# Splitting the attention output on ScalarE and VectorE instead of GpSimd

## The reference, cut to what matters

```python
x = x + cross_attention(layernorm(x), ctx)       # 16 heads, 8192 keys
x = x + self_attention(layernorm(x))             # 16 heads, causal, rotary
x = x + experts(layernorm(x))                    # top 4 of 32, and a shared one

def self_attention(x):                           # x: (512, 512)
    q, k, v = split(x @ w_qkv)                   # 16 heads of 32
    q, k = rotate(q), rotate(k)
    attn = softmax(where(causal, q @ k.T / sqrt(32), -inf))
    out = attn @ v
    return out @ w_o
```

## Time and profile before

| | |
|---|---|
| median of 3 executions | 1501.06 us (1498.43 to 1502.47) |
| the profiled execution, its own time | 1501.06 us |
| its span, first to last instruction | 1499.7 us |
| busy: PE / DVE / ACT / POOL | 95% / 77% / 68% / 42% of the span |
| the chain that ended last, by engine | PE 75%, POOL 10%, DVE 6%, issue 4%, ACT 3%, DMA 2% |
| the units of stage three in the trace | 1208.6 to 1286.2 us |
| product with w_o | from 1288.9 us |

### The profile page before, as it was taken

How to read it: one execution, slowest core, us unless ns; L and a number is a source line. 1 busy time by engine, 2 the same in 40 slices (tenths; PEclk the granted TensorE clock), 3 DMA queues, 4 the chain that set the end, 5 groups by cost and what they waited for, 6 DMA issues and landing times.

```text
span 1499.7 us, 24614 instructions
## 1 busy us (share of the span) xinstructions
PE 1419.0 (95%) x8812; PEld 778.5 (52%) x8812; DVE 1150.2 (77%) x2814; ACT 1017.3 (68%) x1318; POOL 632.5 (42%) x426
## 2 busy tenths in 40 slices
PE   7999999999999976999999999999999899999993
PEld 5866666666666643444444443444443765744441
DVE  6878787887778775899999989998988767533334
ACT  5577777777777775988888888888898446211221
POOL 0199787777787981131152323110000211154551
PEclk9999999999999998999999999999999999999997
DMA  5464344433343235854455444456451340257994
GB/s 197 133 235 155 127 157 165 152 133 128 127 144 138 100 117 162 214 131 116 113 122 129 116 120 112 124 123 169 119 130 40 108 169 1 116 216 271 410 406 175
DMA packets 94574, 229.45 MB, mean 153 GB/s; under 512 B 12737, under 2 KB 13130, under 8 KB 91638
## 3 DMA queue, kind: packets, MB, share of 16 engines
q1 hardware_dynamic: 88288, 218.37, 46.1%
q0 software_dynamic: 5600, 8.42, 1.6%
q10 hardware_dynamic: 566, 1.09, 0.2%
HBM read 171.15 MB, written 64.91 MB: 157 GB/s over the span
## 4 chain that ended last, share of the span: by engine, by line
PE 75%; POOL 10%; DVE 6%; issue 4%; ACT 3%; DMA 2%; SPq 0%; POOLq 0%; ACTq 0%; DVEq 0%
PE PS L796 18%; PE PS L817 15%; PE PS L319 9%; PE PS L323 8%; PE PS L278 5%; PE PS L1623 4%; PE PS L1640 2%; POOL W_ L610 2%; POOL kr L609 2%; POOL kr L612 2%; POOL R L601 2%; PE PS L1582 2%; DVE rel L586 2%; PE PS L825 2%; PE PS L1199 2%
## 5 line engine op out<-in xcount | busy, mean ns | idle before, releaser
L850 ACT ACTIVATE P<-PS 128x1024 f32<-128x1024 f32 x512 | 480.5, 1040 | 81.7 <-PE PS L796 77.9
L586 DVE CUSTOM_DVE_ANT_0 rel<-PS,rel 128x256 f32<-128x256 f32 x1024 | 363.2, 420 | 109.0 <-PE PS L278 105.9
L910 DVE TENSOR_TENSOR W_<-W_,P 128x2048 f32<-128x2048 f32 x108 | 255.2, 2423 | 12.9 <-ACT P L850 12.9
L910 DVE TENSOR_TENSOR acc<-acc,P 128x2048 f32<-128x2048 f32 x108 | 245.4, 2330 | 18.9 <-ACT P L850 18.7
L817 PE MATMUL PS<-P,qe 128*32 128x512 f32 x2048 | 257.0, 600 | 0.7 <-ACT on L873 0.7
L323 PE MATMUL PS<-Wh,R 128*128 128x512 f32 x512 | 180.3, 415 | 0.0
L438 ACT ACTIVATE rel<-PS 128x1024 f32<-128x1024 f32 x128 | 131.5, 1028 | 71.7 <-PE PS L278 71.5
L319 PE MATMUL PS<-R,Wh 128*128 128x512 f32 x512 | 175.6, 414 | 4.1 <-ACT kr L405 4.1
L444 ACT ACTIVATE rel<-PS 128x1024 f32<-128x1024 f32 x128 | 131.5, 1028 | 45.8 <-PE PS L278 45.2
L278 PE MATMUL PS<-khd,qh 32*128 32x256 f32 x2048 | 130.4, 327 | 24.3 <-DVE mpart L586 9.4
L278 PEld LDWEIGHTS PS<-khd,qh 32*128 32x128 f32 x2048 | 79.6, 183 | 123.1 <-issue 81.5
(11 more groups left out here) (304 smaller groups left out, 2078.3 us busy)
## 6 DMA issues: line engine op xcount, KB each, us to landing
khd<-kscr SPq DMA_DIRECT2D x129, 256.0 KB, 4.1
y<-in_y SPq DMA_DIRECT2D x16, 1024.0 KB, 5.4
vscr<-W_ SPq DMA_DIRECT2D x16, 1024.0 KB, 5.0
kscr<-khd SPq DMA_DIRECT2D x16, 1024.0 KB, 7.0
kscr<-kl SPq DMA_DIRECT2D x16, 1024.0 KB, 5.1
qe<-vscr SPq DMA_DIRECT2D x64, 256.0 KB, 2.7
kl<-kscr SPq DMA_DIRECT2D x63, 256.0 KB, 4.2
Wp<-in_w_e SPq DMA_DIRECT2D x6, 1536.0 KB
```

The source lines that it names most:

```text
L586: last = dve.tensor_tensor_reduce(out=rel[i][:, j, t, :], in0=PS[:, 2 * b + j, t * 256:(t + 1) * 256], in1=rel[i][:, j, t, :], scale=1.0, ...
L850: act.activation(P[s % 4][:, 2 * pr:2 * pr + 2, :], PS[:, 2 * b:2 * b + 2, :], ACT.Exp, scale=SCALE).then_inc(exp_done, 1)
L910: dve.tensor_tensor(a[:, :, :], a[:, :, :], P[s % 4][:, :, :], ALU.add).then_inc(summed, 1)
```

## The change

ACT and DVE take over what POOL did for `at_`, and ACT the copies of `w_o`. POOL keeps the four subtractions for `w_o`. ACT now makes the copy for group g at the end of unit 3g + 5 (u = 5, 8, 11), after `take_turned(u - 1)`, and one copy of `w_o` at the end of each of the units 3 to 6, behind the former. DVE makes the subtraction for group g at the end of the same unit, after `empty_turned(u - 1, 0)`, and waits there for ACT's copy. The semaphore `split3` goes; PE waits for `at_low` at 3 and at 4 instead.

```diff
 # third_pe
-        pe.wait_ge(split3, 6)
+        pe.wait_ge(at_low, 3)
         pe.wait_ge(w_lows, 12)
...
-        pe.wait_ge(at_low, 1)
+        pe.wait_ge(at_low, 4)
 # third_act
             if u:
                 take_turned(u - 1)
+            if u > 2 and u % 3 == 2:
+                high_attention(u // 3 - 1)
+            if 2 < u < 7:
+                if u == 3:
+                    act.wait_ge(qw_in, 48)
+                    act.wait_ge(side_made, SIDE["project", 2, 3] + 1)
+                act.copy(R[2][:, u - 3, :], W0[0][:, u - 3, :]).then_inc(wo2_high, 1)
         act.activation(dmy[:, 1:2], epst[:, 0:1], ACT.Sqrt)
         take_turned(11)
         take_shares(3)
-        act.wait_ge(at_done, 4)
-        act.copy(R[0][:, 3, :], at_[:, 3, :]).then_inc(at_high, 1)
+        high_attention(3)
...
+    def high_attention(g):
+        act.wait_ge(at_done, g + 1)
+        act.copy(R[0][:, g, :], at_[:, g, :]).then_inc(at_high, 1)
 # third_dve
             if u:
                 empty_turned(u - 1, 0)
+            if u > 2 and u % 3 == 2:
+                low_attention(u // 3 - 1)
         empty_turned(10, 1)
         empty_turned(11, 0)
         empty_turned(11, 1)
         weighted(3)
-        dve.wait_ge(at_high, 1)
-        dve.tensor_tensor(R[1][:, 3, :], at_[:, 3, :], R[0][:, 3, :].bitcast(F32), ALU.subtract).then_inc(at_low, 1)
+        low_attention(3)
...
+    def low_attention(g):
+        dve.wait_ge(at_high, g + 1)
+        dve.tensor_tensor(R[1][:, g, :], at_[:, g, :], R[0][:, g, :].bitcast(F32), ALU.subtract).then_inc(at_low, 1)
 # third_pool
-        pool.wait_ge(qw_in, 48)
         for k in range(4):
-            pool.tensor_copy(R[2][:, k, :], W0[0][:, k, :]).then_inc(wo2_high, 1)
             pool.wait_ge(wo2_high, k + 1)
             pool.tensor_tensor(R[3][:, k, :], W0[0][:, k, :], R[2][:, k, :].bitcast(F32), ALU.subtract).then_inc(w_lows, 1)
-        for g in range(3):
-            pool.wait_ge(at_done, g + 1)
-            pool.tensor_copy(R[0][:, g, :], at_[:, g, :]).then_inc(split3, 1)
-            pool.wait_ge(split3, 2 * g + 1)
-            pool.tensor_tensor(R[1][:, g, :], at_[:, g, :], R[0][:, g, :].bitcast(F32), ALU.subtract).then_inc(split3, 1)
 # fourth_sp
-        sp.wait_ge(at_low, 1)
+        sp.wait_ge(at_low, 4)
```

More of the change, by code:

```diff
@@ L1058, in program @@
     xT2_dve = sem("xT2_dve")
-    w_lows, split3 = sem("w_lows"), sem("split3")
+    w_lows = sem("w_lows")
     pair_in = [sem(f"pair_in{i}") for i in range(11)]
```

## The result

| | before | after |
|---|---|---|
| median | 1500.37 us (6 runs) | 1515.22 us (6 runs, 1513.55 to 1516.36) |
| ratio, 95% interval | | 1.0099 (1.0087 to 1.0112) |
| profiled execution, its own time | 1501.06 us | 1515.08 us |
| span | 1499.7 us | 1513.7 us |
| mean granted clock of TensorE | 0.983 | 0.976 |

The change makes the kernel about 1% slower, 14.85 us by the medians. The forecast was slower, but by 5.05 us.

A forecast was written before the change was run, and what follows sets the result against it. PE was taken as the bound, busy 16.36 of 16.70 us. Two turns at 1.84 plus 1.37 at the end gave 5.05 us on 1501.06, so 1506.1 us; 8-in-10 range 1502.0 to 1508.8.

The forecast's parts named there:

- Value: The worth set on each part in stage three: POOL's relief 0, ACT's added copies 0.
- Sum: The total over two turns and the end of unit 11: 2 x 1.84 + 1.37 = 5.05 us slower.
- Nothing gained from GpSimd's relief: POOL loses 8.1 us of copies and subtractions before unit 11 ends; nobody waited for them, so 0.
- POOL's work was slowing DVE: Rival: if all 8.1 us of POOL came off DVE's path, 3.1 us net gain, 1498.0 us; chance 4%.
- ScalarE's copies at units 3, 4 and 6: 0: At these unit ends copies push exponentials by up to 0.62 us, which ACT's idle time takes up: 0.
- VectorE's wait and the steps behind it: DVE waits for ACT's late copy ahead of the maxima: 1.84 us at turns 5-6 and 8-9, 1.37 after unit 11.
- The lock with GpSimd: At unit 5 a POOL subtraction could hold up DVE's new one by at most 1.3 us once; taken as 0.
- The delays are not taken up: Against the rival that DVE's waits fall into idle time at the turns: 1501.7, up to 1503.5 us; chance 17%.
- The clock: Rival: PE's gaps bring one clock fall before the product with w_o, 2.5 us more, 1508.6 us; chance 13%.
- The range: The forecast's own range for the whole kernel, 1505 to 1507.8 us, given 60%.

The follow-up runs named there:

- fill_exact: Changed kernel with short fp32r filler products on TensorE that end within its three new gaps; 1504.77 us, ratio 1.0034.
- copy_early: Changed kernel with ScalarE's copy of at_ in units 5, 8 and 11 moved ahead of raise_scores(u, 0); 1500.07 us, ratio 0.9997.
- weight_only: Kernel before with only the four copies of w_o moved to ScalarE, everything for at_ as before; 1499.52 us, ratio 1.0000.
- pool_late: Kernel before with GpSimd's key-weight subtractions held until VectorE's last step of the first normalisation is done; 1501.87 us, ratio 1.0010.
- low_later: Changed kernel with VectorE's subtractions moved behind shift(6, 1), shift(9, 1) and the last copies of turned blocks; 1502.00 us, ratio 1.0008.
- attention_only: Changed kernel with GpSimd keeping its four copies of w_o, so only the at_ work moves; 1512.00 us, ratio 1.0088.
- fill_end: Changed kernel with float32 filler products on TensorE only in the gaps behind unit 11; 1513.03 us, ratio 1.0073.
- wait_only: Kernel before with only a VectorE wait for ScalarE's take_turned(u - 1) at the ends of units 5 and 8; 1502.33 us, ratio 1.0015.
- both: Kernel before with the edits of norm_fill and pool_late together; 1502.83 us, ratio 1.0021.
- norm_fill: Kernel before with fp32r filler products on TensorE in the gaps of the first normalisation; 1500.40 us, ratio 1.0003.

## Why the prediction was wrong

The direction was right, and so was the mechanism of the 5 us that it forecast. Two thirds of the slowdown came by another way, and there one step failed: "Value" and "Sum" took a gap on PE to cost its own length, and left the clock to a rival with 13% and one fall of 2.5 us, "in front of the product". The runs showed three falls, worth 10.2 us beside 4.97 us of lateness (fill_exact).

- **Nothing gained from GpSimd's relief.** Right: copy_early leaves it the whole relief of 8.1 us and stands at 0.9997, weight_only the relief of four copies and stands at 1.0000. The rival "POOL's work was slowing DVE" is refuted.
- **ScalarE's copies at units 3, 4 and 6: 0.** Right within what can be measured (weight_only).
- **VectorE's wait and the steps behind it: 1.84 a turn, 1.37 at the end.** Right. The wait is 2.18 us, the maxima 0.61 behind the subtraction's start, the scores 1.50 behind the exponentials. With the clock held the two periods grow by 1.81 and 1.82 us and the end by 1.34; the sum is 4.97 against 5.05. My working put ScalarE's copy 0.57 behind the start of the last one; it follows 0.46 behind, and takes 0.65 rather than 0.62, so that the wait ends 0.08 us sooner than I had it. And `raise_scores(9, 1)` at 1271.67 does not start "when ACT is free", which would be 1269.93 + 1.45 = 1271.38, but 1.26 behind the start of its maxima at 1270.41; in the changed trace ScalarE indeed waits 0.28 us for them.
- **The lock with GpSimd: 0.** Right. At unit 5 GpSimd's subtraction starts at 1250.65, in the last 0.13 us of VectorE's, and both have their usual durations, 1.26 and 0.69 us. The Trainium skill (SBUF — State Buffer, Who interferes with whom) has a VectorE instruction with two SBUF inputs contend with a GpSimd instruction that reads SBUF; pool_late agrees, with 1.19, 1.79 and 1.67 us for the three two-input steps of the first rotation beside GpSimd, and 0.69 each without it. The two durations that I had called in agreement with it (3.86 and 1.92 us) are of a step with one tensor as input: they show that the engines hold each other up, but are no case of that sentence.
- **The delays are not taken up.** Right: no part of the 5 us is won back up to the product with `w_o` (fill_exact).
- **The clock.** Wrong in number and in place. It fell three times, at both turns and at the end, and cost 10.2 us, twice the lateness. Against it I had set that gaps of 1.53 and 0.90 us after unit 11 "were followed by no fall", and for it only the likeness of the last stretch. That was the wrong row to weigh. The turns' gaps (2.1 by my own working, 1.94 measured) are longer than those, and longer than any in rows 8 too: there no gap of PE was over 1.35 us until the one of 1.74 that ended at 1184.06, and in it the clock fell. At the end of unit 11 the first gap is 1.53 as before; the second one, 1.19 by the late copy, is new, and in it the clock fell. Last, a fall takes more than the 2.5 us read from rows 8, where PE was idle for part of the time and the low stretch went on beyond the two windows: here the low stretches hold 5 to 10 us of work each.
- **The range.** By its own terms, 4.5 to 6.35 us on 1501.06, the forecast's own range is 1505.6 to 1507.4 and not 1505 to 1507.8. This decides nothing.

With that step put right by the rows at hand (a fall of 2.5 us for each of the three new gaps) the same working would have given 5.05 + 7.5 = 12.6 us, 1513.6. With the 22.2 us of work in the low stretches, read only after the fact, it is 5.05 + 11.1 = 16.2 us, against 15.17 between the profiles. How long a fall lasts was not forecast by anything in the trace before.

## What to carry to other kernels

A subtraction of 0.69 us that nobody waits for can still cost microseconds by its place: in an in-order list a wait for a late partner holds everything behind it, here the maxima on which the exponentials and the next scores depend. Move the producer to where its engine is idle (copy_early) or the waiter behind what is urgent (low_later); both brought the 1% back to within 0.1% by their medians. And where TensorE sets the time, price a new gap twice, once for its length and once for what it does to the clock behind it; in the share of busy time the second looks like work, and only the granted clock tells it from work.

## What the runs showed of the hardware

- Behind a gap of 1.93 or 1.94 us ahead of the scores of units 7 and 10 the granted clock was at its lower level in each of the three profiles with such gaps (the changed kernel, attention_only, fill_end); behind one of 0.82 at the same place (wait_only) it stayed at 1.00. With fillers that leave 0.34 (fill_exact) it stayed at 1.00 too. What gaps between 0.82 and 1.93 do there was not tried. The Trainium skill (TensorE: Matmul & The Clock Gate, Part 1) says that the gate goes by how busy TensorE has been recently; these profiles agree.
- The length of the gap alone does not decide. Ahead of `scores(1, 0)` gaps of 1.82 us (the changed kernel), 1.85 (weight_only) and 2.46 (both) were followed by no fall, while one of 1.84 (norm_fill) and one of 3.03 (pool_late) were. In the first normalisation one of 1.74 was (the kernel before), and ones of 1.73 (the changed kernel) and 1.82 (pool_late) were not. What differs was not tried.
- Low stretches come and go with the execution: the first normalisation of the same code had 0.50 for 6 us in the profile of the kernel before and 1.00 in that of the changed one. That such stretches are one source of the 4 to 5 us between runs of one kernel is borne out by the 29 runs of the kernel before that stood beside norm_fill: the 9 with a mean granted clock of 0.982 or less have a median of 1502.0 us, the 9 with 0.985 or more one of 1497.6.
